# Windowed attention with sinks in an eight-layer kernel: another order of the same steps on three engines

## What is computed

```python
proj = x @ W_qkv                      # 32 query heads, 8 key/value heads, 64 features each
q = _apply_rope(q.reshape(B, L, NKV, QM, HD), cos, sin)     # QM = 4 query heads per key head
k = _apply_rope(k.reshape(B, L, NKV, HD), cos, sin)
attn = jnp.einsum('bqhmd,bkhd->bhmqk', q, k) * sm_scale
mask = (q_pos >= k_pos) & (q_pos < k_pos + SW)              # the near 64 keys are masked out
attn = jnp.where(mask, -jnp.inf, attn)
w = jax.nn.softmax(jnp.concatenate([attn, sink], axis=-1), axis=-1)[..., :-1]
out = jnp.einsum('bhmqk,bkhd->bqhmd', w, v).reshape(B, L, NQ * HD)
return out @ W_out
```

## Time and profile before

| what | value |
|---|---|
| median of 3 runs | 4052.7 us (4051.71 to 4053.6) |
| span of the profiled execution | 4055.4 us, 2.7 us above that median |
| mean granted TensorE clock | 0.879 |
| busy: PE, DVE, ACT, POOL | 3283.2, 2809.6, 2274.5, 1766.8 us |
| first batch's attention steps (window 1790 to 2060 us) | PE 265.1, DVE 217.1, ACT 220.4, POOL 138.2 us busy of 270 |

### The profile page before, as it was taken

One profiled execution on the slowest core, in us unless ns is written; L12 is line 12 of the kernel. 1 busy time (PEld: TensorE's weight loads), 2 busy tenths in 40 slices (PEclk: granted clock), 3 DMA queues, 4 the chain that ended last, 5 costly groups with the idle time before them and its releaser, 6 DMA issues. The chain is left out here.

```text
span 4055.4 us, 68591 instructions
## 1 busy us (share of the span) xinstructions
PE 3283.2 (81%) x19700; PEld 2595.3 (64%) x19707; DVE 2809.6 (69%) x6227; ACT 2274.5 (56%) x5958; POOL 1766.8 (44%) x3039
## 2 busy tenths in 40 slices
PE   7799967925888489169999999999957499999575
PEld 3355556714777377058778778778745378888453
DVE  5699966646777666368858858768673378888742
ACT  3599923414777344068858868768602166666211
POOL 0299923567664045635535445446327400000165
PEclk9699977967999689579999999999956599999666
DMA  2011132440000335310000000000053500000435
GB/s 86 20 47 47 49 153 80 137 104 24 1 1 1 148 99 136 98 59 19 19 9 19 20 9 20 17 10 20 16 184 63 119 1 1 1 1 1 160 72 111
DMA packets 139453, 221.35 MB, mean 55 GB/s; under 512 B 28912, under 2 KB 114800, under 8 KB 137408
## 3 DMA queue, kind: packets, MB, share of 16 engines
q1 hardware_dynamic: 108432, 156.23, 11.6%
q0 software_dynamic: 30720, 61.44, 7.3%
HBM read 162.60 MB, written 54.80 MB: 54 GB/s over the span
## 5 line engine op out<-in xcount | busy, mean ns | idle before, releaser
L1242 POOL DMA_INDIRECT ex_xr<-scratch_rows,mo_token x288 | 287.0, 997 | 326.1 <-PE bank L1301 167.7
L596 POOL TENSOR_TENSOR sc_h<-sc_h,sc_c 128x512 f32<-128x512 f32 x256 | 327.0, 1291 | 198.1 <-DVE sc_h L633 190.1
L3034 DVE TENSOR_TENSOR sa_pT<-bank,sa_pT 128x512 fp32r<-128x512 f32 x512 | 329.9, 686 | 34.4 <-ACT sa_pT L2902 30.5
L2894 ACT ACTIVATE sa_p<-bank,sa_nm 128x512 f32<-128x512 f32 x512 | 347.0, 689 | 2.5 <-DVE sa_nm L3025 2.5
L633 DVE TENSOR_TENSOR_SCAN sc_h<-sc_da,bank 128x512 f32<-128x512 f32 x256 | 311.1, 1220 | 39.4 <-ACT sc_da L576 24.5
L2723 PE MATMUL bank<-sa_kT,sa_qT 128*128 128x512 f32 x1024 | 332.5, 436 | 1.5 <-DVE residual L3001 1.5
L3021 DVE TENSOR_REDUCE sa_mx<-bank 128x2 f32<-128x1024 f32 x256 | 312.4, 1220 | 25.7 <-PE bank L2725 22.0
L1319 PE MATMUL bank<-mo_w_gu,ex_xT 128*128 (+2 forms) x1152 | 315.7, 403 | 1.1 <-issue 0.5
L2747 PE MATMUL bank<-sa_pT,sa_v 128*128 128x256 f32 x2048 | 301.5, 290 | 16.9 <-DVE sa_pT L3034 16.5
L2747 PEld LDWEIGHTS bank<-sa_pT,sa_v 128*128 128x128 f32 x2048 | 260.2, 190 | 40.1 <-DVE sa_pT L3034 31.6
L2902 ACT ACTIVATE sa_pT<-bank 128x512 fp32r<-128x512 f32 x512 | 274.3, 585 | 7.9 <-PE bank L2735 0.7
(11 more groups left out here) (401 smaller groups left out, 9405.6 us busy)
## 6 DMA issues: line engine op xcount, KB each, us to landing
scratch_ys<-ex_yo SPq DMA_DIRECT2D x192, 128.0 KB, 2.1
mo_w_gu<-in_w_gu SPq DMA_DIRECT2D x2, 9216.0 KB, 26.8
sc_c<-scratch_c SPq DMA_DIRECT2D x64, 256.0 KB, 3.1
sa_share<-scratch_shares SPq DMA_DIRECT2D x256, 64.0 KB, 2.5
mo_w_dn<-in_w_dn SPq DMA_DIRECT2D x2, 4608.0 KB, 46.5
scratch_rows<-ln_stage SPq DMA_DIRECT2D x64, 128.0 KB, 1.9
mo_w_dn<-in_w_dn SPq DMA_DIRECT2D x2, 4096.0 KB, 34.8
ex_xr<-scratch_rows,mo_token POOLq DMA_INDIRECT x288, 2.8
```

The lines of the kernel that those rows point to most:

```text
L596: pool.tensor_tensor(h, h, C[u], ALU.mult).then_inc(used.sem, 1)
L1242: pool.indirect_dma_start(xr[u][:, :], None, rows, bass.IndirectOffsetOnAxis(ap=token[:, i:i + 1], axis=0), bounds_check=rows.shape[0] - 1 ...
L2894: act.activation(pr[h][:, :], SC[2 * s_ + h][:, :], ACT.Exp, bias=nm[:, col:col + 1], scale=SCALE, accum_out=rs[:, col:col + 1]).then_inc( ...
L3034: dve.tensor_tensor(spot(1), PT[h][:, :].rearrange("p (k n) -> p k n", k=TPB), spot(0).bitcast(F32), ALU.subtract).then_inc(*inc("kept_d"))
```

## The change

On TensorE `turn_p(N-1)` stands directly behind `scores(N)`, ahead of `project` and `values`. On ScalarE `high_p(N-1)` and `exps(N)` stand ahead of `fetch_q` and `low_y(N-2)`. On VectorE `low_p(N-1)` stands ahead of `add_y(N-2)`. No instruction is added, removed or altered, the lists of GpSimd and SP are the same, and what is called at the end of a batch stays as it was.

```diff
--- before.py
+++ after.py
@@ -2763,16 +2763,16 @@
                             if s_ == 1 and (qt + 1 < QUADS or not last):
                                 turn_q(q + 1, qt + 2 < QUADS or not last)
                             scores(g, p)
+                            if p >= 1:
+                                turn_p(N - 1, p - 1)
+                            elif not first:
+                                turn_p(N - 1, p - 1 + STEPS_)
                             if s_ == 0 and (qt + 2 < QUADS or not last):
                                 project(q + 2, *((g, qt + 2) if qt + 2 < QUADS else (g + 1, qt + 2 - QUADS)))
                             if p >= 2:
                                 values(N - 2, g, p - 2, 0)
                             elif not first:
                                 values(N - 2, g, p - 2 + STEPS_, 1)
-                            if p >= 1:
-                                turn_p(N - 1, p - 1)
-                            elif not first:
-                                turn_p(N - 1, p - 1 + STEPS_)
                         if last:
                             N = I * STEPS_ + STEPS_
                             values(N - 2, g, STEPS_ - 2, 0)
@@ -2912,17 +2912,17 @@
                             q = I * QUADS + qt
                             if s_ == 1 and (qt + 1 < QUADS or not last):
                                 keep_q(q + 1, qt + 1)
+                            if p >= 1:
+                                high_p(N - 1, p - 1)
+                            elif not first:
+                                high_p(N - 1, p - 1 + STEPS_)
+                            exps(N, p)
                             if s_ == 0 and (qt + 2 < QUADS or not last):
                                 fetch_q(q + 2)
                             if p >= 2:
                                 low_y(N - 2, p - 2)
                             elif not first:
                                 low_y(N - 2, p - 2 + STEPS_)
-                            if p >= 1:
-                                high_p(N - 1, p - 1)
-                            elif not first:
-                                high_p(N - 1, p - 1 + STEPS_)
-                            exps(N, p)
                             if s_ == 1:
                                 cut = slice((qt % 2) * HG, (qt % 2 + 1) * HG)
                                 act.wait_ge(*at("sunk", q + 1))
@@ -3058,14 +3058,14 @@
                             qt, s_ = divmod(p, 2)
                             q = I * QUADS + qt
                             maximum(N, g, p)
+                            if p >= 1:
+                                low_p(N - 1, p - 1)
+                            elif not first:
+                                low_p(N - 1, p - 1 + STEPS_)
                             if p >= 2:
                                 add_y(N - 2, q - 1, p - 2)
                             elif not first:
                                 add_y(N - 2, q - 1, p - 2 + STEPS_)
-                            if p >= 1:
-                                low_p(N - 1, p - 1)
-                            elif not first:
-                                low_p(N - 1, p - 1 + STEPS_)
                             if s_ == 0 and qt >= 1:
                                 invert(q - 1, qt - 1)
                             elif s_ == 0 and not first:
```

## The result

| | before | after |
|---|---|---|
| median | 4052.97 us (4 runs, 4051.71 to 4053.6) | **4387.02 us** (4 runs, 4384.36 to 4395.53) |
| span of the profiled execution | 4055.4 us | 4384.1 us |
| mean granted clock | 0.879 | 0.865 |

The ratio is 1.0821, with a 95% interval of 1.0808 to 1.0834. The change costs 334 us; 246 were forecast, and the time lies 52 us above the range. From the first L3021 to the last of each of the four batches the sums are 941.7 us before and 1266.5 after, so 324.7 of the 328.7 us by which the span grew lie between these instructions, inside the stage that was spoken of. Of the other 4.0 us, 2.5 lie ahead of the first L3021, which is no larger than what one execution differs from another.

The account below looks back on a forecast made before the run. TensorE was taken to set the attention's pace; new waiting loops raise a quad from 7.48 to 9.54 us, 61.5 us a batch, 246 for four. 4052.7 + 246 = 4299 us, range 4225 to 4335.

Parts of the forecast that it names:

- The new pattern, 76% busy: TensorE in the changed attention, idle some 2.2 us in one piece before turn_q; no clock loss was charged.
- the row with 2.75 of 4 us busy: A stretch of the rotary attention, ahead of this one, granted clock 1.00; the prediction compared the new pattern with it.
- Rival 4: TensorE's clock falls in the new gap, doubling turn_q and scores: 11.3 us a quad, about 4510 us; chance 0.06.
- The full-clock quad: Two attention steps, an even and an odd one: forecast 9.54 us against 7.48 before.
- The even chain: Even step's loop from maximum through exps, fetch_q, turn_q and scores to the next maximum: 5.11 us.
- The odd chain: Odd step's loop from maximum through exps, low_y and add_y to the next maximum: 4.43 us with the GpSimd hold.
- The wait at turn_q: TensorE waits for fetch_q before turn_q, some 2.2 us 116 to 120 times, about 260 us in all.
- GpSimd's hold of the negation: L2554 holds the shared port and delays the negation L3025 by 0.43 us in every odd step.
- rival 2: Both chains bind, but the negation slips by GpSimd: 9.11 us a quad, 4246 us; chance 0.14.
- high_p costs nothing: High_p ahead of exps on ScalarE: less than 0.1 us lost in the odd step, nothing charged, 0.1 kept for the range.
- Rival 1: TensorE's waits vanish and nothing else is on the path: faster, 4029 us; chance 0.06.
- the granted clock of 1.00: Sign that the forecast was right: TensorE's granted clock stays at 1.00 in the changed attention.

Follow-up runs that it names:

- e2: The changed kernel with 16 small matmuls, whose result nobody reads, ahead of each turn_q that waits for fetch_q: 4322.0 us.
- e7: The kernel before with TensorE's exchange alone, turn_p(N-1) ahead of project and values(N-2): 4341.4 us.
- e5: The kernel before with one call moved on ScalarE, fetch_q behind exps: 4383.0 us.
- e1: The changed kernel with one call put back on ScalarE, fetch_q ahead of exps again: 4114.3 us.
- e4: The changed kernel with 16 small matmuls ahead of turn_q and GpSimd's last put_q pass made to wait for the negation: 4282.2 us.
- e6: The kernel before with VectorE's exchange alone, low_p(N-1) ahead of add_y(N-2): 4154.6 us.
- e3: The changed kernel with one wait more on GpSimd, put_q's last pass waiting for the odd step's negated maximum: 4334.4 us.

## Why the prediction was wrong, and where it was right

**The step that failed:** "The new pattern, 76% busy, resembles the first more than the second, so I charge nothing." The clock did fall, in 54 of the 120 quads with a gap, and that costs 63 to 65 us (e2 against the changed kernel). Without it the time would have been 4322 us, inside the range. The error lay in the comparison: the row with 2.75 of 4 us busy gave a mean over a stretch, and the new pattern has its idle time in one piece of 2.07 us ahead of dense work, which a share of busy time doesn't tell from many small gaps. That the one piece is what matters is likely, not shown. e7, 82% busy with gaps of 1.1 us at most, kept a clock of 1.00; the changed kernel's quad at 2200.30 is 79% busy (7.64 of 9.71 us) with one gap. But e2 changed the gap and the share together, and in e5 a longer gap, 2.44 us, let the clock fall less often. Rival 4 had the mechanism and a chance of 0.06, and its sign came, scores that take nearly twice as long behind the gap; but it priced the clock at 1.76 us in all 120 quads, 211 us. Measured: 54 quads at 1.43 to 1.48 in the even step, less 0.4 that the odd one gives back, since the negation escapes L2554, and a shorter fall in the third quad of two batches. So the rival was on the list, with its condition and its place, and the right size was neither 0 nor 211 us.

**Terms that were mis-sized:** of the loops' 262 us the sum had 246. The full-clock quad is 9.70, where 9.54 stood. The even chain was 5.10 to 5.18 for 5.11: turn_q to scores took 0.39 behind a wait in place of 0.35, scores 1.35 in place of 1.41, mostly since the mask's product has 128 columns in that quad and 256 in the row. The odd chain was 4.51 to 4.61 for 4.43, and nearly all of it is one link: low_y starts 0.79 us behind the second exponential's start (2208.00 to 2208.79), where 0.66 was taken from the exponential ahead of keep_q. 120 x 0.16 = 19 us, inside the 36 that the range kept for it.

**What held.** The loops are where they were said to be: 120 waits in front of turn_q ended by fetch_q, add_y's wait of 1.0 us in nearly every step. e1 removes the first and keeps the second, as its chain says. The wait at turn_q was 1.92 us on average, 230.6 in all, for a forecast of 2.2 and 260: it is 2.07 in front of the slow even steps and where the clock is full for several quads, 1.80 to 1.91 in the quad behind a slow one, whose odd step is shorter, and 0.7 to 0.8 in each batch's second quad. GpSimd's hold of the negation is real and 0.40 us (0.43 in the sum); e4 shows it by taking it away, so rival 2 is out, though in the changed kernel itself about half the odd steps escape the hold behind a slow even step. high_p costs nothing: it is done at 2206.93, 0.39 ahead of the exponentials. Rival 1 fell: by the prediction's sum its condition missed by a microsecond, and TensorE stood 2.07 us.

**Signs that were listed and did not come:** the granted clock of 1.00, L3025 of 0.6 us in every odd step, and ScalarE's busy time unchanged. The latter rose by 37 us though its instructions' mean durations stayed as they were (L2902 588 ns for 585). Records of instructions that follow directly overlap (two copies L2902 of 0.588 us fill 1.06 us in e6's row), and in the new order more of them stand alone; that would lengthen the counted time, but no run tested it.

## What to carry over

Measure a new order by its loops: for each moved instruction ask what it waits for now and whether that, some links on, waits for it; then add the links from start to next start, with the handover each engine needs. When a loop opens a gap of about 2 us in front of TensorE (here 1.85 to 2.44 us were enough), look at the granted clock behind every such gap and price both levels, since the work behind the gap is by construction on the loop. Moving work ahead on one engine only pays if what it feeds on is ready there, and in this kernel the copy that frees a bank had to go ahead of the long work of its step.

## What the runs showed of the chip beyond what was expected

- The clock falls behind some gaps and not behind equal ones. Every second quad was slow in two batches from the start, behind gaps of 2.07 us with 1.81 between them; in the other two only from the eighth quad on, and their fifth to seventh quads have gaps of 2.05 to 2.07 us too, with full clock behind them. With a gap of 2.44 us and a quad of 10.0 (e5) it was about every fifth, and with one of 1.85 to 1.90 us and a quad of 9.3 (e3) irregular. So the gap's length alone doesn't decide, and what does was not settled; that work in the gap prevents it was (e2, e4).
- 16 matmuls of 128 columns, 1.07 us in all, in a gap of some 2.2 us, kept the clock at 1.00 and gave 63 to 65 us back.
- A copy of 64 partitions (low_y) starts 0.79 us behind the start of the exponential ahead of it, one of 128 partitions (fetch_q, 2203.10) 0.66 behind its own (2202.44); the cause of the 0.13 us is open.
- A slower link can repay part of itself: the slow even step moved the next negation past GpSimd's L2554 and made the odd step 0.4 us shorter.
